# A recurrent layer with a gated feed-forward on eight cores: the second half of the layernorm is emitted later, and residual loads and output stores move from the GpSimd queue to the SyncE queue

## The reference, cut to what matters

```python
xn = layernorm(x)
# recurrent branch
gate, xa = split(xn @ w_in.T)
xc = causal_conv4(xa) + b_conv
forget, inp = split(xc @ w_gates.T + b_gates)
alpha = exp(-8 * softplus(forget_base) * sigmoid(forget))
u = sqrt(1 - alpha**2 + 1e-6) * sigmoid(inp) * xc
h[t] = alpha[t] * h[t-1] + u[t]
s = (gelu(gate) * h) @ w_out.T
# selected feed-forward: 8 candidates for each output
logits = xn @ sel_w.T + sel_b        # 1024 x 8
comp   = xn @ comp_w.T + comp_b      # 8 x 1024
g = silu(comp[argmax(logits)])
out = x + s * g
```

## Time and profile before

| | us |
|---|---|
| median of three runs | 4184.94 |
| lowest and highest of them | 4117.46, 4332.98 |
| the profiled execution, its own time | 4117.57 |
| its span on the slowest core (first to last instruction) | 4115.7 |
| spans of the eight cores | 4105.4 to 4115.7 |
| TensorE busy | 3623.4 (88%) |
| VectorE busy | 1541.7 (37%) |
| GpSimd busy | 1547.8 (38%) |
| ScalarE busy | 1141.1 (28%) |

### The profile page before, as it was taken

The page is one execution under the profiler, slowest core; times in us unless marked ns, Lnnn a source line. Parts: engine busy times, 40 slices in busy tenths (PEclk is TensorE's granted clock), DMA queues, the critical chain, the costliest instruction groups (busy, mean ns, idle before and its releaser), DMA issues.

```text
span 4115.7 us, 46749 instructions; the slowest of 8 cores (4105.4 to 4115.7 us)
## 1 busy us (share of the span) xinstructions
PE 3623.4 (88%) x16272; PEld 1605.8 (39%) x16272; DVE 1541.7 (37%) x1696; ACT 1141.1 (28%) x1331; POOL 1547.8 (38%) x816
## 2 busy tenths in 40 slices
PE   2998999997489899999658989999965999999994
PEld 0443444442234344444223434444422444444442
DVE  2415334533232533443423253344342335344333
ACT  1333222222133322222213432222221343222221
POOL 1433444441233444444123344444413444444442
PEclk8999999998799999999879999999987999999997
DMA  2333333331223333333122223333312222333331
GB/s 73 93 98 92 102 101 101 103 103 51 92 84 99 95 103 103 103 102 103 42 92 93 92 93 102 103 103 103 103 41 92 92 93 92 103 103 103 103 103 51
DMA packets 362775, 380.61 MB, mean 92 GB/s; under 512 B 12304, under 2 KB 356384, under 8 KB 362544
## 3 DMA queue, kind: packets, MB, share of 16 engines
q1 hardware_dynamic: 354816, 352.36, 27.5%
q0 software_dynamic: 7728, 25.27, 2.0%
HBM read 369.20 MB, written 8.39 MB: 92 GB/s over the span
## 4 chain that ended last, share of the span: by engine, by line
PE 75%; DVE 10%; POOL 4%; DMA 4%; ACT 3%; issue 3%; DVEq 0%; POOLq 0%; ACTq 0%
PE pg L273 74%; DMA poolA<-xT 3%; POOL wl L86 3%; DVE poolC L86 3%; DVE poolB L86 2%; DVE hb L86 1%; ACT wh L86 1%; PE pg L340 1%; PE pg L334 1%; DVE mxb L86 1%; DVE msk L86 1%; DVE xnl L86 1%; DVE accb L86 1%; ACT sf L86 0%; DVE scr L86 0%
## 5 line engine op out<-in xcount | busy, mean ns | idle before, releaser
L86 POOL TENSOR_TENSOR wl<-w,wh 128x1024 bf16<-128x1024 f32 x672 | 1472.1, 2191 | 2197.8 <-ACT wh L86 2147.7
L273 PE MATMUL pg<-xnh,wh 128*128 128x512 bf16 x4608 | 1765.4, 383 | 274.7 <-POOL wl L86 251.2
L273 PE MATMUL pg<-xnl,wh 128*128 128x512 bf16 x4608 | 1764.3, 383 | 0.0
L273 PE MATMUL pg<-xnh,wl 128*128 128x512 bf16 x4608 | 1762.8, 383 | 0.0
L86 ACT ACTIVATE wh<-w 128x1024 bf16<-128x1024 f32 x672 | 710.1, 1057 | 1649.5 <-PE pg L273 1611.1
L273 PEld LDWEIGHTS pg<-xnh,wh 128*128 128x128 bf16 x4608 | 454.4, 99 | 840.3 <-issue 308.7
L86 DVE TENSOR_SCALAR si<-pg,vecsb 128x512 f32<-128x512 f32 x256 | 192.2, 751 | 1388.2 <-PE pg L273 1386.8
L273 PEld LDWEIGHTS pg<-xnh,wl 128*128 128x128 bf16 x4608 | 454.7, 99 | 556.1 <-issue 21.8
L273 PEld LDWEIGHTS pg<-xnl,wh 128*128 128x128 bf16 x4608 | 454.3, 99 | 550.6 <-issue 18.0
L273 PE MATMUL pg<-xch,wh 128*128 128x512 bf16 x768 | 298.7, 389 | 93.7 <-POOL wl L86 93.7
L273 PE MATMUL pg<-xcl,wh 128*128 128x512 bf16 x768 | 298.1, 388 | 0.0
(11 more groups left out here) (58 smaller groups left out, 834.0 us busy)
## 6 DMA issues: line engine op xcount, KB each, us to landing
w<-selT SPq DMA_DIRECT2D x256, 512.0 KB, 5.0
w<-cmpT SPq DMA_DIRECT2D x256, 512.0 KB, 5.1
w<-w1T SPq DMA_DIRECT2D x64, 512.0 KB, 5.4
w<-w2T SPq DMA_DIRECT2D x64, 512.0 KB, 5.1
w<-w3T SPq DMA_DIRECT2D x32, 512.0 KB, 4.9
hb<-xT POOLq DMA_DIRECT2D x32, 256.0 KB, 3.6
poolA<-xT POOLq DMA_DIRECT2D x32, 256.0 KB, 3.9
outT<-poolC POOLq DMA_DIRECT2D x32, 256.0 KB, 2.5
```

The costliest lines, as they stand in the source:

```text
L86: return fn(*a, **k)
L273: last = tensor.matmul(bank[:, :], wop[:, wcol:wcol + P], xop[:, k * TT:(k + 1) * TT], start=(idx == 0), stop=(idx == 23))
```

## The change

It has two parts. First, `emit_LN` is cut in two. Its first part (sums, small chain) stays where it was. The second part, `emit_LN_post` (the two spreading matmuls and the 32 VectorE instructions), is emitted behind the second group of `w_out`. Second, the loads of x and the stores of the output in the output loop are issued by SyncE and no more by GpSimd, with the same waits.

```diff
@@ in emit_LN
                 brow_tok = ("sc", c.inc(ins, "sc"))
+                return (rstd_tok, brow_tok)
+
+            def emit_LN_post(t):
+                rstd_tok, brow_tok = ln_rows_box[0]
+                R = lambda j: rows[:, j * TT:(j + 1) * TT]
                 bA, bB = next_bank(), next_bank()
                 c.needt(tensor, "pe", rstd_tok)
                 c.needt(tensor, "pe", brow_tok)
...
-            xn_rdy_box = [emit_LN(0)]
+            ln_rows_box = [None]
+            ln_rows_box[0] = emit_LN(0)
+            xn_rdy_box = [None]
+            xn_rdy_box[0] = emit_LN_post(0)
...
                     if i == 7 and t + 1 < nt:
-                        xn_rdy_box[0] = emit_LN(t + 1, preloaded=True)
+                        ln_rows_box[0] = emit_LN(t + 1, preloaded=True)
...
                     if m % 2 == 1:
                         whl_free[par] = gtok
                         load_next_half()
+                    if m == 1 and t + 1 < nt:
+                        xn_rdy_box[0] = emit_LN_post(t + 1)
...
                 for i in range(8):
                     xsl = i % 2
-                    c.needt(gpsimd, "gp", free_A[xsl])
-                    ins = gpsimd.dma_start(
+                    c.needt(sync, "sync", free_A[xsl])
+                    ins = sync.dma_start(
                         out=poolA[:, xsl * TT:(xsl + 1) * TT],
                         in_=xT[i * P:(i + 1) * P, t0:t0 + TT])
...
-                    c.need(gpsimd, "gp", "ve", otok[1])
-                    ins = gpsimd.dma_start(
+                    c.need(sync, "sync", "ve", otok[1])
+                    ins = sync.dma_start(
                         out=outT[i * P:(i + 1) * P, t0:t0 + TT], in_=OBi)
```

## The result

The changed kernel takes 3953.5 us in the median of ten runs. Against the kernel before, the ratio is 0.9587, with a 95% interval from 0.9575 to 0.9599: faster by 4.1%. The profiled execution took 3953.46 us, against 4117.57 before: 164 us less. The forecast was 3965 with a range from 3905 to 4050.

The account below looks back on a forecast made before the run. VectorE's order with the output loop in it was taken to set when a tile begins. Gains of 43.9 us at three places and 18.9 at the last tile's end, 151 in sum, took 4117.57 to 3966.9, said as 3965; range 3905 to 4050.

Parts of the forecast that it names:

- What sets the begin of a tile: Between tiles: VectorE's order, with the output loop in it, sets when a tile begins; TensorE has slack there.
- Selection chain first: VectorE after tile 0: the chain starts at 983.95 without the 5.3 us wait, ends at 1004.1, 28.5 us earlier.
- the convolution's loss three times: VectorE's 32 xnh/xnl instructions: three GpSimd splits beside them cost 3.38 us each, 10.1 together; bounds nothing or 13.9.
- The 1.5 us for the first product and sum: Start of the output loop: loss to the split of the second half running beside them; bounds 0 and 4.6.
- The round on SyncE: Output loop: one round takes 5.0 us, with a load of 3.6, against 5.8 on GpSimd; bounds 4.3 and 7.2.
- 3 x 43.9 + 18.9 = 151: Total gain in us: 43.9 at each of three places between tiles, 18.9 at the end of the last tile.
- (a): Rival, between tiles and at the end: transfers no faster from SyncE, splits shut VectorE out fully; 4016 us, chance 0.16.
- (c): Rival, between tiles and at the end: full loss to splits and rounds of 7.2 us; 4055 us, chance 0.06.
- (b): Rival, between tiles and at the end: no loss to splits, rounds of 4.3 us; 3910 us, chance 0.12.
- (d): Rival, 28 later output-loop rounds: loads and stores land late on SyncE's queue; slower, 4200 us or more, chance 0.02.
- (e): Rival, VectorE's order: something taken as ready makes VectorE wait as long as before; 4117 us, chance 0.02.
- The overlap of the parts: Both parts, whole kernel: reordering alone gains 85 us, SyncE alone 144, together 151 and not 229.

Follow-up runs that it names:

- post_m5: The changed kernel with the second half of the layernorm emitted behind the sixth group of w_out instead of the second: 4013.4 and 4014.7 us.
- prefetch2: The changed kernel with x loads issued two rounds ahead and a product waiting only for the store two rounds back: 3893.0 and 3890.4 us.
- sync_only: The kernel before with the output loop's loads and stores issued by SyncE instead of GpSimd, layernorm in one piece: 4007.2 and 4010.1 us.
- sync_hoist: sync_only with the first load of x of each output loop issued ahead of w_out: 3999.0, 3996.9, 3999.5 us; ratio 0.9704.
- sync_woven: sync_hoist with rounds 0 and 1 of the output loop emitted between the groups of w_out: 3977.7, 3979.8, 3978.0 us; ratio 0.9639.

## Why the prediction was right, point by point

**What sets the begin of a tile.** VectorE's order with the output loop in it: shown by `post_m5`, where only VectorE's start moves and the kernel takes 60 us more, and by `prefetch2`, where only the loop's transfers move and it takes 61 less.

**Selection chain first.** Forecast to end 20.15 us behind the small chain, at 1004.1 on the old clock. It ends at 996.39 + 5.74 = 1002.13, 19.8 behind 982.33. Right.

**Splits beside the 32 instructions.** I took the convolution's loss three times, 10.1 us. Measured: from 1002.23 to 1030.56 + 0.69 = 1031.25, 29.0 us, less 23.2, so 5.8. This step was mis-sized. Three splits did run beside the 32 instructions:

```profile
1005.07 9.19 POOL L86 TENSOR_TENSOR wl<-w,wh 128x1024 bf16<-128x1024 f32 x4 [40.05 <-ACT wh L86]
...
1023.21 4.58 POOL L86 TENSOR_TENSOR wl<-w,wh 128x1024 bf16<-128x1024 f32 x2 [8.96 <-ACT wh L86]
```

Each stretched one `xnl` by 1.7 us (0.69 to 2.42) and the cast to `xnh` before it by 0.15 to 0.33; the two instructions that read PSUM take 0.69 each, also while GpSimd runs its splits from 1005.07 to 1014.26. The rule of the Trainium skill (SBUF — State Buffer, Who interferes with whom), by which I had given half of 10.1, agrees with that. The 1.5 us for the first product and sum were nothing: they ended at 1032.84, and the split began at 1033.57.

**The round on SyncE.** Forecast 5.0 us; measured 5.25, 6.13, 5.64 and, in the last tile, 5.30. The issue terms were right:

```profile
1059.23 0.69 DVE L86 TENSOR_TENSOR poolC<-poolC,poolA 128x512 f32<-128x512 f32 x1 [0.71 <-DMA poolA<-xT]
```

```profile
1060.00 0.34 SPq L708 DMA_DIRECT2D outT<-poolC  x1
1060.39 0.42 SPq L685 DMA_DIRECT2D poolA<-xT  x1
```

From the sum's end to the store's issue there are 0.08 us (GpSimd: 0.57), and the load's issue begins 0.39 later (0.54). On this core, the slowest, the load was the mis-sized term: 3.6 forecast, and the page of the changed kernel has

```profile
poolA<-xT SPq DMA_DIRECT2D x32, 256.0 KB, 4.2
outT<-poolC SPq DMA_DIRECT2D x32, 256.0 KB, 2.6
```

in the median, with loads of 3.4 in some rounds and up to 5.7 in others. In the second place, with loads of 4.3 to 5.7, the round was even longer than the 5.8 of before. But this core is not like the rest. In the same profile the median load is 3.4 to 3.6 us and the median store 2.3 on cores 2 to 7 (4.1 and 2.5 on core 0), while all eight cores of the kernel before have 3.9 or 4.0 and 2.5. So the 3.6 was right for six cores and too low for the slowest; as a mean over the eight cores a round takes 5.3 us, where it took 5.9.

The other rule of the Trainium skill that I weighed (DMA: Bandwidth & Descriptors, Issuing engines are not separate DMA queues) says that only the issue time is saved. The trace agrees for the larger part: around the issues a round saves 0.57 + 0.54 less 0.08 + 0.39 = 0.64 us. It does not agree to the letter: on cores 2 to 7 the load, counted from the start of its issue, also lands 0.3 to 0.6 us sooner than from GpSimd, of which the shorter issue (0.42 against 0.54) is 0.12.

**The sum.** 3 x 43.9 + 18.9 = 151 forecast; 132.8 + 20.0 = 152.8 measured between the same marks. That this is so near is in part luck: the loss to splits was 4.3 too high at each place, the 1.5 came to nothing, and seven rounds at 0.25 to 1.13 us too low took that back. The result lies 13 us under the 3966.9 of the sum: 2 from the terms, and 11 are the rest named above, 6 of it at the program's end, for which the forecast had no term.

**Rivals.** (a) and (c) needed the full shut-out or slow loads; the shut-out was 5.8 of 13.9. (b) needed none. (d), the late landing on SyncE, did not decide, but it is the one that had something in it: rounds up to 6.13. (e) is out: the 43.21 us wait is gone.

**The overlap of the parts: wrong.** I had SyncE alone at 144 us, so that the reordering would add 7. Measured: reordering alone 83 at the three places and 2 in the last tile, SyncE alone 84 and 20, together 132.8 and 20. So the reordering adds 49 to SyncE. The step that failed is "SyncE alone would let the first sum end at 1034.21 + 1.6": the first sum ended at 1053.87 in `sync_only`. For both parts together I had looked at what stands ahead of the loop on SyncE (the load of the third half, free at about 1016), but I carried the answer over to the old order, where the splits come late. `sync_hoist` and `sync_woven` show this: with the loads and stores moved past the waiting weight loads, 29 us of the 49 come back without any change in the order of VectorE or TensorE. The other 20 are not separated by a run: 3 lie ahead of the first product and 17 in the rounds. What the reordering does for the path is therefore not to bring VectorE's first product forward: at the first place this comes 49.7 us behind the small chain's last row instead of 50.9 (1034.21 - 983.27), because the waits that go, 5.3 us for the matmuls and 1.64 for `al`, are nearly eaten by the 5.8 us lost to splits. It puts the splits, and with them the weight loads that wait on SyncE or the splits that GpSimd has ahead of the loop, under the 32 instructions, so that the loop finds its queue free. SyncE's timeline in the changed kernel has the last weight load ahead of the loop over, and the first load of x issued, 17 us before VectorE wants it at 1032.15:

```profile
965.09 50.15 SPq L212 DMA_DIRECT2D w<-w1T  x6
1015.35 0.44 SPq L685 DMA_DIRECT2D poolA<-xT  x1
```

## What to carry to other kernels

Where engines take their work strictly in order, write down for each queue what stands ahead of a moved DMA as well as behind it, and when the wait of the instruction ahead ends; a move between queues is worth what the new neighbours let it be worth. A loop of load, sum and store with waits in series costs its latencies, not its bytes: load two rounds ahead and wait only for the slot's own store. When two edits touch one path, estimate each alone and test both: here, between the marks, the parts alone gave 86 and 104 us, 190 in sum, and both together gave 153.

## What the runs showed of the hardware that I had not expected

The weight loads between 1040 and 1200 us landed later after the change: the longest took 8.1 to 12.6 us on the eight cores, against 5.8 to 8.3 before, with no more bytes in all (380.61 MB in both pages). Whether the loads now meet each other, or those of other cores, was not tried. The slowest core of the changed kernel's profile is also the one whose weights land late throughout: its median for the pieces from `selT` is 5.8 us, on the seven others it is 4.6 to 4.9, and 4.5 to 5.0 on all eight before. So a median of the slowest core is not the chip's. And the program's end came 6 us sooner when the last transfers were issued from SyncE, in each of the seven kernels of this kind that I looked at; the cause is open.
